# The second attention of a fused two-block kernel in cycles of four tiles

## What is computed

```python
def _topk_cross_attn(h, ctx, w_q, b_q, w_kv, b_kv, w_co, b_co):
    q = (h @ w_q + b_q).reshape(B, L, H, D)
    kv = (ctx @ w_kv + b_kv).reshape(B, Lc, 2, H, D)
    k, v = (kv[:, :, 0], kv[:, :, 1])
    scores = jnp.einsum('bqhd,bkhd->bhqk', q, k) / jnp.sqrt(jnp.float32(D)).astype(h.dtype)
    top_s, top_i = jax.lax.top_k(scores, TOPK)
    attn = jax.nn.softmax(top_s, axis=-1)
    v_bh = jnp.transpose(v, (0, 2, 1, 3))
    vg = jnp.take_along_axis(v_bh[:, :, None, :, :], top_i[..., None], axis=3)
    o = jnp.einsum('bhqk,bhqkd->bqhd', attn, vg).reshape(B, L, C)
    return o @ w_co + b_co
```

## Time and profile before

| | us |
|---|---|
| three runs | 1635.76, 1636.42, 1628.56 (median 1635.76) |
| the profiled execution | 1626.4 |
| its span, first to last instruction | 1624.6 |

### The profile page before, as it was taken

How to read it: one execution, slowest core, us unless ns; L and a number is a source line. 1 busy time by engine, 2 the same in 40 slices (tenths; PEclk the granted TensorE clock), 3 DMA queues, 4 the chain that set the end, 5 groups by cost and what they waited for, 6 DMA issues and landing times.

```text
span 1624.6 us, 25766 instructions
## 1 busy us (share of the span) xinstructions
PE 1427.5 (88%) x9132; PEld 725.4 (45%) x9132; DVE 912.2 (56%) x2815; ACT 697.8 (43%) x1370; POOL 386.3 (24%) x632
## 2 busy tenths in 40 slices
PE   5999857778968977789989999999999998998898
PEld 3567645454644644334223333333333254454565
DVE  2455457776877876566546666667576235450121
ACT  2245433445335434113554465555545753434221
POOL 0010057775776776200000000000010001010110
PEclk9899957769979978799999999999999999999999
DMA  5022100000000000100002000000000000000000
GB/s 177 1 85 80 51 1 14 8 1 1 2 4 1 2 27 2 34 1 1 1 1 66 1 1 1 1 1 1 1 11 1 1 2 1 12 4 2 14 22 21
DMA packets 22095, 26.77 MB, mean 16 GB/s; under 512 B 4204, under 2 KB 19634, under 8 KB 21708
## 3 DMA queue, kind: packets, MB, share of 16 engines
q1 hardware_dynamic: 21059, 25.03, 4.8%
q10 hardware_dynamic: 909, 0.10, 0.0%
HBM read 21.58 MB, written 3.08 MB: 15 GB/s over the span
## 4 chain that ended last, share of the span: by engine, by line
PE 55%; DVE 3%; ACT 3%; issue 2%; POOL 1%; ACTq 0%; POOLq 0%; DVEq 0%
PE bank L930 25%; PE bank L968 8%; PE bank L887 7%; PE bank L902 5%; PE bank L866 3%; PE bank L845 2%; PE bank L971 1%; PE bank L824 1%; PE bank L973 1%; PE bank L852 1%; ACT pr L1154 1%; DVE part_max L1361 1%; PE bank L831 1%; ACT h_t L1096 1%; DVE x_hat L1334 1%
## 5 line engine op out<-in xcount | busy, mean ns | idle before, releaser
L1154 ACT ACTIVATE pr<-bank 128x512 f32<-128x512 f32 x656 | 354.9, 597 | 322.6 <-PE bank L930 322.5
L1361 DVE TENSOR_REDUCE part_max<-bank 128x1 f32<-128x512 f32 x512 | 327.6, 685 | 195.4 <-PE bank L930 194.5
L930 PE MATMUL bank<-slot 32*128 32x512 f32 (+1 forms) x3072 | 392.0, 526 | 6.3 <-ACT pr L1154 4.8
L930 PEld LDWEIGHTS bank<-slot 32*128 32x128 f32 x3072 | 153.8, 187 | 220.3 <-issue 171.8
L1411 POOL TENSOR_SCALAR var_eps<-mean_var 128x4 f32<-128x4 f32 x24 | 5.5, 229 | 1010.5 <-DVE mean_var L1325 1010.4
L1171 ACT ACTIVATE exp_all<-bank,neg 128x154 f32<-128x154 f32 x256 | 85.5, 389 | 147.9 <-POOL neg L1456 141.4
L1470 POOL TENSOR_SCALAR left<-left 128x308 f32<-128x308 f32 x128 | 126.3, 987 | 75.7 <-issue 48.4
L887 PE MATMUL bank<-h_t,w_m 128*128 128x512 f32 x256 | 131.3, 638 | 7.7 <-DVE hidden L1341 5.0
L968 PE MATMUL bank<-pr,v 128*17 128x512 f32 x1024 | 136.5, 605 | 0.0
L1386 DVE MAX8 top<-bank 128x8 f32<-128x154 f32 x256 | 69.6, 313 | 68.6 <-PE bank L992 64.8
L1473 POOL TENSOR_TENSOR probs<-left,exp_all 128x256 f32<-128x256 f32 x128 | 93.6, 731 | 0.0
(11 more groups left out here) (140 smaller groups left out, 1945.7 us busy)
## 6 DMA issues: line engine op xcount, KB each, us to landing
w_m<-in_L_xcond_w_m SPq DMA_DIRECT2D x1, 2048.0 KB, 7.8
w_m<-in_L_xcond_w_m SPq DMA_DIRECT2D x2, 1024.0 KB, 6.9
w<-in_L_xcond_w SPq DMA_DIRECT2D x2, 1024.0 KB, 6.5
w_ada<-in_L_xcond_w_ada SPq DMA_DIRECT2D x1, 1792.0 KB, 10.7
x_sb<-in_x SPq DMA_DIRECT2D x6, 256.0 KB, 7.3
res_row<-rows_dram SPq DMA_DIRECT2D x12, 128.0 KB, 3.4
out_x<-x_sb SPq DMA_DIRECT2D x6, 256.0 KB, 2.1
wa<-in_L_xcond_w_qkv SPq DMA_DIRECT2D x1, 768.0 KB, 8.0
```

The source lines that it names most:

```text
L930: last = nc.tensor.matmul(g.bank(*tile)[:, into], left, right, start=True, stop=True)
L1154: nc.scalar.activation(m.pr[:, u % NPR, :], g.bank("s", gi, i)[:, :], ACT.Exp).then_inc(g.free("s", gi, i), 1)
L1361: nc.vector.tensor_reduce(m.part_max[:, slot, h * TB + i // 8, i // 4 % 2:i // 4 % 2 + 1], bank[:, :], axis=AX.X, op=ALU.max).then_inc(don ...
```

## The change

- `c_neg` moves to ScalarE, as a copy with scale -1.
- `c_pick` multiplies marks and exps of all 154 tokens in one instruction; `probs` has 160 columns a head and `tails` goes.
- `c_tail` becomes four plain products with the identity, side by side, into a quarter of bank 7, the values' bank. The first of four tiles waits for the `o_copy` of the four tiles before. Bank 6 goes to the token work, in place of bank 1, which goes to the scores.
- `c_copy` fills a quarter of a `probs_t` for four tiles, which lies where the values of batch 1 of attentions 1 and 3 lie; at the fourth tile it also copies bank 7 to `tails_t`. `c_pv` runs once for four tiles, with 512 columns. The values of (4, 1) may be written only after group 15; GpSimd fills their ones anew at `reload`.
- `topk_run` plans by tiles: scores 0.8 of a tile ahead, transposes 1.9 tiles after the tile's start. The token work is laid in slots by `under`, one a tile for (2, 1), two a tile for (3, 0) and (4, 0), with steps of ScalarE 0.4 and of VectorE 0.9 of a tile after the slot's time. In (3, 0) silu comes in two pieces a block.
- Attention 3 starts 0.3 of a tile after the planned end, and the token work under it four slots later.

The diff, cut to its core:

```diff
-        return (2, 3, 4)
+        return (1, 2, 3, 4)
     if kind == "c_turn":
         return (5,)
-    if kind == "c_tail":
-        return (6,)
     if kind == "o_turn":
-        return (0, 1) if attention(step[1]) == 2 else (0, 1, 2)
+        return (0, 6) if attention(step[1]) == 2 else (0, 1, 2)
...
+ON_SCALAR = ("on_copy", "modulate", "ua_copy", "silu", "qk_a", "v_copy")
+ON_VECTOR = ("x_sum", "stats", "rstd", "x_hat", "hid", "qk_d", "out_sum")
...
+            for step in steps:
+                self.at(time + (later[0] if step[0] in ON_SCALAR else later[1] if step[0] in ON_VECTOR else 0.0), step)
...
-        tail[-1] += [("silu", s, b, n, q) for q in range(4)]
+        tail = gap + [[("ua", s, b, n, j), ("ua_copy", s, b, n, j)] for j in range(HT)]
+        for j in ((HT - 1,) if b else (3, HT - 1)):
+            tail[j + apart] += [("silu", s, b, n, q) for q in range(j // 4 * 2 * (1 - b), (j + 1) // 2)]
...
-                    plan.at(start + (v - 1.1) * step, ("c_score", gi, t, 0), ("c_score", gi, t, 1), ("c_scores", gi, t))
+                    t0 = start + u * step
+                    plan.at(t0 - 0.8 * step, ("c_score", gi, t, 0), ("c_score", gi, t, 1), ("c_scores", gi, t))
                     for hf in range(2):
-                        t0 = start + v * step
-                        plan.at(t0, ("c_top", gi, t, hf), ("c_neg", gi, t, hf))
-                        plan.at(t0 + 0.5 * step, ("c_exp_all", gi, t, hf))
-                        plan.at(t0 + 1.0 * step, ("c_pick", gi, t, hf))
-                        v += 1
-                    t1 = start + v * step
-                    plan.at(t1 + 0.55 * step, ("c_tail", gi, t), ("c_turn", gi, t))
-                    plan.at(t1 + 0.85 * step, ("c_copy", gi, t))
-                    plan.at(t1 + 1.25 * step, ("c_pv", gi, t))
+                        t1 = t0 + 0.5 * hf * step
+                        plan.at(t1, ("c_top", gi, t, hf))
+                        plan.at(t1 + 0.12 * step, ("c_neg", gi, t, hf))
+                        plan.at(t1 + 0.25 * step, ("c_exp_all", gi, t, hf))
+                        plan.at(t1 + 0.55 * step, ("c_pick", gi, t, hf))
+                    plan.at(t0 + 1.9 * step, ("c_tail", gi, t), ("c_turn", gi, t))
+                    plan.at(t0 + 2.0 * step, ("c_copy", gi, t))
                     if t % 4 == 3:
-                        plan.at(t1 + 1.6 * step, ("o_copy", gi, half))
-                        plan.at(t1 + 2.0 * step, ("o_turn", gi, half))
-                        plan.at(t1 + 2.4 * step, ("o_norm", gi, half))
-    return start + 128 * step
+                        plan.at(t0 + 2.3 * step, ("c_pv", gi, half))
+                        plan.at(t0 + 2.75 * step, ("o_copy", gi, half))
+                        plan.at(t0 + 3.1 * step, ("o_turn", gi, half))
+                        plan.at(t0 + 3.6 * step, ("o_norm", gi, half))
+                    u += 1
+    return start + u * step
...
-    plan.spread(token_slots(2, 1), A2 + 5, A2 + 37 * step)
     plan.at(A2 + 4, ("load_gate", 3), ("load_w", "m2a"), ("gate_m2", 0))
-    plan.at(A2 + half, ("load_row", 2), ("load_gate", 4), ("load_out", 3), ("gate_out", 3), ("load_gate", 5), ("load_row", 3))
-    plan.at(A2 + 50 * step, ("load_w", "wb1"))
-    three = [block_slots(3, 0, n) for n in range(2)]
-    plan.spread(three[0][0] + three[0][1], A2 + half + 6 * step, A2 + 2 * half + 6 * step)
-    plan.spread(three[1][0] + three[1][1], A2 + 2 * half + 6.1 * step, A2 + 3.5 * half)
-    plan.at(A2 + 3.5 * half, ("load_row", 4), ("load_w", "m2b"), ("gate_m2", 1))
-    plan.spread(token_slots(4, 0), A2 + 3.5 * half + 0.1, A2 + 4 * half - 2 * step)
-    T = end + 3.5 * step
+
+    def under(first, last, slots, per):
+        return plan.fill(slots, [A2 + (first + (i + 0.3) / per) * step for i in range(int((last - first) * per))], (0.4 * step, 0.9 * step))
+
+    under(1, 18, joined([gap_slots(2, 1, n) for n in range(2)]), 1)
+    plan.at(A2 + 18 * step, ("load_row", 2), ("load_gate", 4), ("load_out", 3), ("gate_out", 3), ("load_gate", 5), ("load_row", 3))
+    plan.at(A2 + 19 * step, ("load_w", "wb1"))
+    under(19, 36, in_turn([gap_slots(3, 0, 0, 1)]), 2)
+    under(36, 53, in_turn([gap_slots(3, 0, 1, 1)]), 2)
+    plan.at(A2 + 54.5 * step, ("load_row", 4), ("load_w", "m2b"), ("gate_m2", 1))
+    under(53, 64, joined([gap_slots(4, 0, n, 1) for n in range(2)]), 2)
+    T = end + 0.3 * step
     plan.at(T, ("reload",), ("load_row", 5), ("load_out", 4))
     plan.at(T + 20, ("tails_set",))
     R0, R1 = 2.6, 1.75
     W0, W1 = ROUNDS[3] * R0, ROUNDS[3] * R1
     A3 = T + 0.1
     end, gaps = group_run(plan, 3, A3, R0, R1)
-    early = [gaps[c] + 0.1 * x for c in range(-3, 28, 2) for x in range(2)] + [gaps[c] for c in range(29, 121, 2)]
+    early = [gaps[c] + 0.1 * x for c in range(1, 28, 2) for x in range(2)] + [gaps[c] for c in range(29, 121, 2)]
...
-    m.probs = scratch("probs", [P, 2, HG, P])
-    m.tails = scratch("tails", [P, 2, HG, HW])
-    m.probs_t = scratch("probs_t", [P, (HG + 1) * P])
+    m.probs = scratch("probs", [P, 2, HG, P + HW])
+    m.tails_t = scratch("tails_t", [P, 512])
+    m.probs_t = nc.alloc_sbuf_tensor_at("probs_t", [P, HG, 512], F32, offset=place["v1"])
...
-            nc.tensor.transpose(bank[:, 0:P], m.tails[:, u % 2, :, :].rearrange("p h e -> p (h e)"), m.ident[:, :]).then_inc(m.turned, 1)
+            if t % 4 == 0:
+                since(pe, (m.o_copied, plan.n("o_copy", gi, t // 4)))
+            for h in range(HG):
+                last = nc.tensor.matmul(m.bank[7][h * HW:(h + 1) * HW, t % 4 * P:(t % 4 + 1) * P], m.probs[:, u % 2, h, P:P + HW], m.ident[:, :],
+                                        start=True, stop=True, skip_group_check=True)
+            last.then_inc(m.turned, 1)
...
-            pe.wait_ge(*g.freed("c_turn", gi, t))
-            if t % 4 == 0:
-                since(pe, (m.o_copied, plan.n("o_copy", gi, half)))
-            out = m.bank[7][:, t % 4 * P:(t % 4 + 1) * P]
-            nc.tensor.matmul(out, m.vt[:, b, gi % GB, :], m.probs_t[:, HG * P:], start=True, stop=False, skip_group_check=True)
+            pe.wait_ge(*g.freed("c_turn", gi, 4 * half + 3))
+            pe.wait_ge(m.tails_copied, nth + 1)
+            out = m.bank[7]
+            nc.tensor.matmul(out[:, :], m.vt[:, b, gi % GB, :], m.tails_t[:, :], start=True, stop=False, skip_group_check=True)
             for h in range(HG):
-                last = nc.tensor.matmul(out[h * HW:h * HW + VE, :], m.vc[:, b, gi % GB * HG + h, :], m.probs_t[:, h * P:(h + 1) * P],
+                last = nc.tensor.matmul(out[h * HW:h * HW + VE, :], m.vc[:, b, gi % GB * HG + h, :], m.probs_t[:, h, :],
                                         start=False, stop=True, skip_group_check=True)
...
-                act.wait_ge(*g.group_end(3 + 4 * b))
+                act.wait_ge(*g.group_end(15 if b else 3))
...
+        elif kind == "c_neg":
+            v = plan.order[step]
+            act.wait_ge(m.picked, 4 * v + 2)
+            since(act, (m.all_done, v - 3))
+            nc.scalar.activation(m.neg2[:, v % 4, :], m.top[:, v % 2, :, 0], ACT.Copy, scale=-1.0).then_inc(m.neg_done, 1)
...
-            if u:
-                act.wait_ge(m.pv_done, plan.n("c_pv", gi, t))
-            nc.scalar.activation(m.probs_t[:, HG * P:], g.bank("c_tail", gi, t)[:, 0:P], ACT.Copy).then_inc(g.free("c_tail", gi, t), 1)
-            nc.scalar.activation(m.probs_t[:, 0:HG * P], g.bank("c_turn", gi, t)[:, :], ACT.Copy).then_inc(g.free("c_turn", gi, t), 1)
+            if t % 4 == 0:
+                act.wait_ge(m.pv_done, plan.n("c_pv", gi, t // 4))
+            here = slice(t % 4 * P, (t % 4 + 1) * P)
+            if t % 4 == 3:
+                nc.scalar.activation(m.tails_t[:, :], m.bank[7][:, :], ACT.Copy).then_inc(m.tails_copied, 1)
+            nc.scalar.activation(m.probs_t[:, :, here], g.bank("c_turn", gi, t)[:, :].rearrange("p (h t) -> p h t", h=HG),
+                                 ACT.Copy).then_inc(g.free("c_turn", gi, t), 1)
...
+        elif kind == "reload":
+            pool.wait_ge(*g.group_end(15))
+            nc.gpsimd.memset(m.v[1][:, :, :, D:VE], 1.0).then_inc(m.consts, 1)
...
-            left, weights = m.left2[:, v % 4, :, :], m.exp_all[:, v % 4, :, :]
+            left = m.left2[:, v % 4, :, :]
             nc.gpsimd.tensor_scalar(left, left, -FAR, None, ALU.is_equal).then_inc(m.marked, 1)
             pool.wait_ge(m.marked, v + 1)
-            nc.gpsimd.tensor_tensor(m.tails[:, u % 2, hh, 0:TAIL], left[:, :, P:S2], weights[:, :, P:S2], ALU.mult)
-            nc.gpsimd.tensor_tensor(m.probs[:, u % 2, hh, :], left[:, :, 0:P], weights[:, :, 0:P], ALU.mult).then_inc(m.pick_done, 1)
+            nc.gpsimd.tensor_tensor(m.probs[:, u % 2, 2 * hf:2 * hf + 2, 0:S2], left, m.exp_all[:, v % 4, :, :], ALU.mult).then_inc(m.pick_done, 1)
```

70 lines of the change are left out of this document (34 added, 36 removed).

## The result

Measured: 1604.7 us, median of four runs (1601.97 to 1609.24), against 1634.4 us for the kernel before (1628.56 to 1636.42). The ratio is 0.983, interval 0.980 to 0.986: 30 us faster. Forecast were 1551 us, 1515 to 1600; the time lies 54 us above the forecast and 5 us outside the range. The profiled execution took 1604.1 us.

The account below looks back on a forecast made before the run. A loop through GpSimd was taken to bound the second attention's 442 us. The stage was to take 114 + 246 = 360 us, 82 less, the seam 3 less: 1541 us profiled, plus 9.4 to the median, 1551 us; range 1515 to 1600.

Parts of the forecast that it names:

- The loop of before: Second attention: negation, exps and marks through in-order GpSimd take 3.10 us a half-tile, with other work 421 of 442 us.
- The terms of the loads: Second attention after the change: TensorE 320 us, VectorE 325, ScalarE 208, GpSimd 270; negation 0.2 us, product 0.84.
- The front: Second attention's first 20 tiles: 5.7 us a tile, the middle of VectorE's 4.95 and 6.4 at the low clock.
- rival A: Second attention: VectorE runs gap-free, 330 us, time 1518 us, or 1537 at 5.4 a tile; chance 0.18.
- Behind it, 44 tiles: Second attention after the first 20 tiles: VectorE's 5.14 us a tile plus 9% for stalls, 5.6, 246 us.
- rival B: Second attention: TensorE sets the pace through stage 3's side units and VectorE's follow-ups, 6.0 us a tile, 1590 us; chance 0.15.
- rival E: Second attention: ScalarE's copy waiting for TensorE stands ahead of each negation and recloses the loop, 6.7 a tile, 1623 us; chance 0.04.
- the tail products: Second attention, TensorE: the tails' transpose (21.6 us) becomes four plain products, about 29.7 us, 8 us more.
- The silu cut: Stage 3, batch 0: silu in two pieces per block adds table loads of 1.28 us on ScalarE, 5 us more.
- The seam: End of the second attention: the third's first maxima start 7.5 us earlier, gaining 3 us, bounds 0 and 8.
- The signs: Right if VectorE is busy over 88% and GpSimd's picks near 2.8 us; wrong if VectorE waits over 60 us for scores.
- D, the lock: Second attention: GpSimd's instructions block VectorE's second replacement, 0.9 us each; gain of 2 us, 1634 us; chance 0.01.

Follow-up runs that it names:

- neg_alone: The kernel before with only the negation moved from GpSimd to ScalarE, in the old order with old banks and two products: 1614.97 us, ratio 0.990.
- less_search: The changed kernel with the second MAX8 left out, so only 8 of the 16 scores are found: 1596.59 us, ratio 0.979.
- copy_later: The changed kernel with ScalarE's copy of the transposes planned 0.3 of a tile later, value products and their copy 0.15 and 0.05: 1590.27 us, ratio 0.974.

## Why the prediction was wrong

**The loop of before: right, but not alone.** GpSimd's round with the negation in it cost time: without it the old kernel is 16 us faster, with it the new one 45 slower. But the old order had a second loop right behind (`neg_alone`: the wait moved to ScalarE's copy), and the forecast put the whole old pace down to the first. The terms of the loads came out: negation 203 ns (0.2 taken), product 837 ns (0.84), tail products 29.8 us (29.7), value products 38.4 us (34.5), all four engine sums within 4%.

**The front: right in kind, too dear.** 5.7 a tile were taken, in the middle between VectorE's load and TensorE at the low clock; 5.24 came (VectorE busy 91.48 of 101.7 us), near rival A's case, though `less_search` shows that VectorE was not the only limit there. Worth 25.7 us where 23 were forecast.

**The step that failed: "Behind it, 44 tiles: VectorE 226.09/44 = 5.14; I add 9% for the stalls of rival B, 5.6."** It came to 6.78, which is 53 us over the 45 tiles. In the profiled execution the miss is 62.7 us (1604.1 against 1541.4): these 53.4, 9.0 behind tile 64 and 3 of the seam, less 2.7 that the front did better. (By the medians it is 54, since the profiled execution of before lay 8 us under its own median and that of after did not.) A full engine's load plus an allowance can't price a stretch in which four fixed orders wait for each other. In the old kernel this stretch had run at 6.9, which the forecast put down to GpSimd's loop alone; with that loop gone a second one lay right behind it. Two parts of the miss are sized. First, rival E's place: ScalarE's copy stood ahead of the negation and waited for TensorE. It got a chance of 0.04 and a pace of 6.7 for all tiles; it held behind the front alone (6.78), where ScalarE's wait for transposes was 78.5 us, and moving the copy gave 14 us. Second, the tail products, "8 us more" on an engine that was not the bound: they were indeed some 9 us more (29.8 against 20.6), but on the way from marks through transposes to the next scores, and cost 11 us. Both repairs together took 21 us off, 19 of them in the 45 tiles: 19 of the 53. For the other 34 the step fails without a cause shown.

**Rival B: the nearest time, for a reason that the runs don't bear out.** Its 1590 us was nearest (its own sum of 6.0 a tile gives 1586; it was added up with 6.1), but its loop went through the units of 1.98 us and VectorE's follow-ups. Units cut to half or a quarter gave 2 to 3 us (4 to 6 over the 45 tiles), earlier follow-ups 3 over the 45 tiles and nothing in all. Those cuts let the clock fall, so its price can't be read from them fully.

**Costed at next to nothing.** The silu cut was costed at 5 us of ScalarE; on top of `copy_later` it gains a few. The seam: the first maxima of the third attention came 3.3 us behind tile 64 where they had come 11.6 behind it, but its first value product followed tile 64 by 106.8 us before and 106.9 after, so the 3 us of the seam came to nothing. And the third attention and what follows took 9 us more, for which 0 to 3 were allowed. That isn't the noise of one execution: behind tile 64 the four kernels in the old order take 979 to 984 us, the sixteen in the new one 984 to 992. TensorE is busy 10.6 us more there. From its first value product to its last the third attention took 3.7 us more, from there to the fourth's last 3.2, and what follows 1.9. In the last two TensorE's busy time grew by 3.2 and 1.7 us, with as many instructions, at a granted clock of 0.98 and 0.97 where it had been 1.00 and 0.98: these 5 us go with the clock. What lowers it, and which moved step costs the rest, wasn't tried.

**The signs.** Product, negation and the transposes' wait for products (70.2 us before, 23.0 now) came as forecast, and the first maxima came within 5 us of the last pick. But VectorE was busy 81% of the stage and not over 88%, GpSimd's marks still waited 47.1 us for exps, and from pick to pick GpSimd took 2.5 us in the front and 3.4 behind it, around the 2.8 forecast for both. Of the signs of being wrong, one came, the stage after 650 us that has grown; VectorE's wait for scores stayed under the 60 us named.

**D, the lock.** It priced the wrong instruction: the replacement, which isn't held up, and not the normalisation, which is (last section).

**Open.** With both repairs 45 tiles still take 285.6 us, 6.3 a tile, with TensorE and VectorE busy 240 and 235 us, at a granted clock of 0.88. 32 us less of TensorE gave 7 on top of `copy_later`. What closes the remaining loop isn't shown.
